# A vision-transformer tower on one Trainium2 core: VectorE normalises directly behind the first two row maxima of a step, and GpSimd splits two patch tiles at the end of step 5

## The chip, the cores and the metric

The kernel is one program on one core of a Trainium2 chip. The metric is device time in microseconds (us). PE is TensorE, DVE is VectorE, ACT is ScalarE, POOL is GpSimd and SP is SyncE, which here only issues DMAs. Each engine works through its own instructions in order; semaphores tie the engines together.

## What is computed

```python
patches = _patchify(x)                                   # 64 images, 196 patches of 768
h = einsum('bnf,ef->bne', patches, W_tok) + b            # to 192 features
xn = layernorm(layernorm(h)) * ln_g + ln_b
q, k, v = split(xn @ qkv_w.T + qkv_b)                    # 12 heads of 16
attn = einsum('bhnd,bhmd->bhnm', q, k) * 16 ** -0.5
attn = attn - 0.2 * (sum of the 8 neighbours in the 196 x 196 plane)
h = h + einsum('bhnm,bhmd->bhnd', softmax(attn), v)
...
h = h + experts(layernorm(h))                            # 8 experts, the best 2 per row, 768 hidden
```

## The kernel before, in words

There are two phases. The attention phase takes the images in 32 pairs. The expert phase behind it routes the rows and multiplies them by the experts' weights; the change does not touch it.

**Steps.** A pair has 6 steps, k = 0 to 5: two images times three groups of four heads. Two pairs are one body, whose steps are kk = 0 to 11; bodies 2 to 13 are a hardware loop, the others are written out. "Even pair" below is the one of kk 0 to 5, "odd pair" that of kk 6 to 11. In kk 8, 9 and 11 a body also splits a part of the experts' weights (`stage` to `pack`): ScalarE the high part, VectorE (L838, L840) and GpSimd (L1266) the low parts. Several steps are in flight. In step kk the engines do, in this order:

- TensorE: the scores of heads 0 and 1 of step kk+2 (L635, into `s_bank`); `mix`, probabilities times v of step kk-1 (L664); `transpose_back` of step kk-2 (L617, into `m_bank`); the scores less their maximum of step kk, heads 0 and 1 (L651, `t_bank`); the scores of heads 2 and 3 (L635); a piece of another pair's projections; L651 for heads 2 and 3; `transpose_max` (L675), which turns the maxima of step kk+1 into rows; and once more a piece of projections. In k = 5 that last piece is `project_qk` of the pair after next (L580 to L584): 15 matmuls of 392 columns in three blocks, with nothing between them and the scores of the next step.
- VectorE: `row_maxima` of heads 0 and 1 of step kk+2 (two L859); a piece that depends on k; `normalise` of step kk-2 (L882 the reciprocal of the sums, L886 the product into `att`); `row_maxima` of heads 2 and 3; `split_maxima` (L867 and L870); another piece that depends on k.
- ScalarE: exponentials (L1060), copies out of PSUM and the high parts of splits (`x_hi` L1038, `x_ah` L1090, `x_b` L1092, `padded` L1104, `qk_hi` L1113).
- GpSimd: k = 0 `beside` (L1236) and patch tile 3; k = 1 `sum_rows`; k = 3 patch tile 0, `inverse_deviation` (L1201 to L1207) and `layernorm` (L1212, L1218); k = 4 patch tile 1, `inverse_deviation_n` (L1248 to L1255) and `low_rows` (L1261); k = 5 patch tile 2; kk = 11 also L1266. A patch tile is one `split_patches` (L1228, `x_lo` from `x_buf` and `x_hi`).

**Three ties matter.** `transpose_max` writes the bank that `normalise` reads, so it waits in each step for that step's L886 (`att_ready`). `project_qk` waits for `split_low` (`x_split`): VectorE's L927 and L928 of step 5. `split_low` waits for `x_high`, ScalarE's L1090 and L1092 of the end of step 4:

```python
pe.wait_ge(max_parts_ready, st.s + 1)      # transpose_max
wait(pe, att_ready, st.s - 2)
...
pe.wait_ge(x_split, 4 * (pr.u + 1))        # project_qk, block 0
...
dve.wait_ge(x_high, 2 * (pr.u + 1))        # split_low
```

SP stores and stacks q and k between k = 1 and k = 3 of a pair; the change moves no DMA in SP's queue, and GpSimd issues none in this phase.

Of the kernel before, what the change touches and what calls it, by code (L numbers as in the profile page):

```python
# [84 lines left out]
def wait(eng, sem, value):  # L85

    if not isinstance(value, int) or value > 0:
        eng.wait_ge(sem, value)
# [66 lines left out]
def attention_phase(nc, x_t, w_tok, w_qk_a, w_qk_b, w_v_a, w_v_b, b_tok, b_qk, b_v, ln_cols, row_consts, ident_in,  # L155
# [4 lines left out]
    with ctx:  # L160
# [6 lines left out]
        def sem(name):  # L167
            return ctx.enter_context(nc.semaphore(name))
# [113 lines left out]
        x_split = sem("x_split")  # L282
# [465 lines left out]
        def _(dve):  # L748
# [106 lines left out]
            def row_maxima(st, heads):  # L855
                if st.there:
                    for hh in heads:
                        dve.wait_ge(s_ready, HG * st.s + hh + 1)
                        nc.vector.reduce_max(row_max[st.odd][:, :, hh:hh + 1], s_bank[hh % 2][0:HALF, :, 0:TOKENS],  # L859
                                             AX.X).then_inc(max_ready, 1)  # L860
# [13 lines left out]
            def normalise(st):  # L874

                if st.there:
                    dve.wait_ge(back_ready, st.s + 1)
                    wait(dve, att_ready, st.s)
                    if st.first:
                        wait(dve, y_stored[st.q], 16 * st.before)  # L880
                        wait(dve, xn_n_ready, TILES * (st.pair - 1))
                    nc.vector.reciprocal(recip[:], back_tr[:, :, :, HEAD_DIM:HEAD_DIM + 1]).then_inc(recip_ready, 1)  # L882
                    dve.wait_ge(recip_ready, st.s + 1)
                    width = HG * HEAD_DIM
                    out = att[st.q][:, 2 * st.image:2 * st.image + 2, st.group * width:(st.group + 1) * width]
                    nc.vector.tensor_tensor(out.rearrange("p u (h d) -> p u h d", h=HG),  # L886
                                            back_tr[:, :, :, 0:HEAD_DIM],
                                            recip[:].to_broadcast([HALF, 2, HG, HEAD_DIM]), ALU.mult
                                            ).then_inc(att_ready, 1)
# [33 lines left out]
            def split_low(pr):  # L923

                if pr.there:
                    dve.wait_ge(x_high, 2 * (pr.u + 1))
                    nc.vector.tensor_tensor(x_al[:], xt_a[:], x_ah[:], ALU.subtract).then_inc(x_split, 2)  # L927
                    nc.vector.tensor_tensor(x_b[HI:P, :], xt_b[HI:P, :], x_b[HI:P, :], ALU.subtract  # L928
                                            ).then_inc(x_split, 2)
# [39 lines left out]
            def fill_pipeline():  # L969

                first, second = Pair(0, 0, 0), Pair(0, 0, 1)
                for half in range(2):
                    take_h(first, half)
                    statistics(first, half)
                take_xt_a(first)
                split_low(first)
                for half in range(2):
                    take_h(second, half)
                    statistics(second, half)
                add_tilde(first)  # L980
                take_v(first, 0)
                take_v(first, 1)
                take_low_plain(first)
                take_low_tilde(first)
                take_xt_a(second)
                split_low(second)
                set_up_rows()

            def step(body, kk):
                k = kk % STEPS  # L990
                if kk == -FILL:
                    fill_pipeline()
                row_maxima(Step(body, kk, LOOK), (0, 1))
                if kk >= 0:
                    if k == 1:
                        take_low_plain(Pair(body, kk, 1))
                    elif k == 2:
                        take_h(Pair(body, kk, 2), 0)
                        statistics(Pair(body, kk, 2), 0)
                    elif k == 4:  # L1000
                        take_v(Pair(body, kk, 1), 0)
                        take_v(Pair(body, kk, 1), 1)
                    elif k == 5:
                        split_low(Pair(body, kk, 2))
                normalise(Step(body, kk, -2))
                row_maxima(Step(body, kk, LOOK), (2, 3))
                split_maxima(Step(body, kk, LOOK))
                if kk >= 0:
                    if k == 0:
                        add_tilde(Pair(body, kk, 1))  # L1010
                    elif k == 1:
                        take_low_tilde(Pair(body, kk, 1))
                    elif k == 2:
                        take_h(Pair(body, kk, 2), 1)
                        statistics(Pair(body, kk, 2), 1)
                    elif k == 3:
                        statistics_n(Pair(body, kk, -1))
                    elif k == 4:
                        take_xt_a(Pair(body, kk, 2))
                    if kk == 11:  # L1020
                        low_part(body)
                    if kk == 4 and isinstance(body, int) and body == 1:
                        split_biases()
                    if kk == 10 and isinstance(body, int) and body == 0:
                        prepare_router()
# [169 lines left out]
        def _(pool):  # L1195
# [26 lines left out]
            def split_patches(pr, tiles):  # L1222

                if pr.there:
                    for tile in tiles:
                        cols = slice(tile * HALF, (tile + 1) * HALF)
                        pool.wait_ge(x_hi_ready, TILES * pr.u + tile + 1)
                        nc.gpsimd.tensor_tensor(x_lo[:, :, cols], x_buf[pr.q][:, :, cols], x_hi[:, :, cols],  # L1228
                                                ALU.subtract).then_inc(x_lo_ready[tile // 2], 1)
# [27 lines left out]
            def low_rows(pr):  # L1257
                if pr.there:
                    pool.wait_ge(row_hi_ready, pr.u + 1)
                    wait(pool, row_stored[pr.q], 16 * pr.before)  # L1260
                    nc.gpsimd.tensor_tensor(row[pr.q][:, :, DIM:XROW], xn_n[:], row[pr.q][:, :, 0:DIM], ALU.subtract  # L1261
                                            ).then_inc(row_lo_ready, 1)
# [6 lines left out]
            def step(body, kk):  # L1269
                k = kk % STEPS  # L1270
                if kk == -FILL:
                    first, second = Pair(0, 0, 0), Pair(0, 0, 1)
                    split_patches(first, (0, 1, 2, 3))
                    split_patches(second, (0, 1))
                    pool.wait_ge(consts_set, CONSTS)
                    inverse_deviation(first)
                    layernorm(first)
                    split_patches(second, (2, 3))
                    add_beside(first)
                    inverse_deviation(second)  # L1280
                    layernorm(second)
                    pool.wait_ge(setup_n, 4)
                    nc.gpsimd.affine_select(router.before[:], router.ones[:], [[1, P]], ALU.is_gt, 0.0, base=0,
                                            channel_multiplier=-1).then_inc(before_set, 1)
                if k == 0:
                    add_beside(Pair(body, kk, 1))
                    if Pair(body, kk, 1).there:
                        pool.wait_ge(tilde_ready, Pair(body, kk, 1).u + 1)
                    split_patches(Pair(body, kk, 2), (3,))
                elif k == 1:  # L1290
                    if Pair(body, kk, 1).there:
                        pool.wait_ge(plain_lo_ready, Pair(body, kk, 1).u + 1)
                    sum_rows(Pair(body, kk, -1))
                elif k == 3:
                    split_patches(Pair(body, kk, 3), (0,))
                    if kk >= 0:
                        inverse_deviation(Pair(body, kk, 2))
                        layernorm(Pair(body, kk, 2))
                elif k > 3:
                    split_patches(Pair(body, kk, 3), (k - 3,))  # L1300
                    if kk >= 0 and k == 4:
                        inverse_deviation_n(Pair(body, kk, -1))
                        low_rows(Pair(body, kk, -2))
                if kk == 11:
                    low_part(body)
            run_bodies(pool, step)


# [727 lines left out]
```

## Time and profile before

| | us |
|---|---|
| median of three runs (lowest, highest) | 2218.97 (2218.96, 2224.03) |
| the profiled execution | 2227.03 |
| its span | 2225.0 |
| PE, DVE busy | 1889.0 (85%), 1496.4 (67%) |
| ACT, POOL busy | 1274.4 (57%), 1136.7 (51%) |
| granted TensorE clock, mean | 0.922 |

The shares are means over two unlike phases. The attention phase ends near 1250 us of the span and the expert phase takes up its speed near 1400 us. A granted clock of 1.00 is 2.4 GHz, 0.50 is 1.2 GHz.

### The profile page before, as it was taken

To read this page: it belongs to the slowest core of one execution; us is meant where nothing else is said; L and a number is where in the kernel's file an instruction comes from. 1 tells how busy PE (TensorE), PEld (TensorE's weight loads), DVE (VectorE), ACT (ScalarE), POOL (GpSimd) and SP (SyncE) were. 2 spreads that over 40 slices of the span, in tenths; PEclk is the share of its full clock that TensorE was granted. 3 is DMA by queue.
4 is the path that set the end of the run, shared out by engine and by line. 5 is a ranking of instruction groups with operands and counts; after the bars stand their busy time and mean duration, and the time that the engine had idled before them with its cause. 6 is when DMAs were issued, how large, how long until landed. Compare 5 with 4: busy or idle time off the path is not lost. (4 is left out here: it accounts for less than half of the span.)

```text
span 2225.0 us, 54385 instructions
## 1 busy us (share of the span) xinstructions
PE 1889.0 (85%) x17949; PEld 1396.1 (63%) x17949; DVE 1496.4 (67%) x4652; ACT 1274.4 (57%) x2469; POOL 1136.7 (51%) x1069
## 2 busy tenths in 40 slices
PE   4878888888888878788888657999999999999991
PEld 4655565656565656565655445777777777777761
DVE  4768787888788888888888534655655655654430
ACT  4657777777777777777777623444444444433330
POOL 4335454444545454545453234666676676664442
PEclk8889999999999999999998756999999999999996
DMA  4565555555556454645463326887888888789886
GB/s 151 159 192 160 161 178 157 176 162 165 170 155 183 143 176 157 185 143 169 160 184 114 112 85 163 200 190 201 214 189 208 209 188 207 197 198 176 187 165 191
DMA packets 362727, 382.72 MB, mean 172 GB/s; under 512 B 144532, under 2 KB 326096, under 8 KB 358288
## 3 DMA queue, kind: packets, MB, share of 16 engines
q1 hardware_dynamic: 320912, 338.66, 52.1%
q0 software_dynamic: 41664, 42.12, 11.2%
q8 instruction: 86, 1.41, 0.3%
q14 instruction: 65, 0.53, 0.1%
HBM read 232.83 MB, written 135.46 MB: 166 GB/s over the span
## 5 line engine op out<-in xcount | busy, mean ns | idle before, releaser
L859 DVE TENSOR_REDUCE row_max<-s_bank 98x2 f32<-98x392 f32 x768 | 395.3, 557 | 110.0 <-PE s_bank L635 109.6
L1790 DVE SCALAR_TENSOR_TENSOR ml<-mid_bank,mh 128x512 bf16<-128x512 f32 x336 | 232.1, 691 | 329.3 <-ACT mh L1878 328.2
L1878 ACT ACTIVATE mh<-mid_bank 128x512 bf16<-128x512 f32 x336 | 200.7, 597 | 409.4 <-PE mid_bank L1569 409.4
L1060 ACT ACTIVATE probs<-t_bank 98x392 f32<-98x392 f32 x768 | 342.5, 503 | 121.2 <-PE t_bank L651 119.6
L1944 POOL DMA_INDIRECT sums<-y_out,tail x168 | 265.2, 1578 | 158.0 <-DVE y_out L1820 110.9
L1586 PE MATMUL y_bank<-wst,ml 128*128 128x192 bf16 x1344 | 330.1, 246 | 0.0
L1583 PE MATMUL y_bank<-wst,mh 128*128 128x192 bf16 x1344 | 330.1, 246 | 0.0
L1585 PE MATMUL y_bank<-wst,mh 128*128 128x192 bf16 x1344 | 329.9, 245 | 0.0
L1228 POOL TENSOR_TENSOR x_lo<-x_buf,x_hi 128x588 f16<-128x588 f32 x128 | 172.0, 1346 | 298.2 <-ACT x_hi L1038 234.0
L635 PE MATMUL s_bank<-k_stack,q_stack 96*98 96x196 f16 x1536 | 224.4, 257 | 48.7 <-DVE row_max L859 38.0
L651 PE MATMUL t_bank<-q_stack,k_stack 104*98 104x196 f16 x1536 | 224.2, 258 | 40.2 <-ACT probs L1060 36.5
L1929 POOL DMA_INDIRECT slots<-row_r,spot x196 | 191.2, 975 | 98.8 <-issue 56.4
L635 PEld LDWEIGHTS s_bank<-k_stack,q_stack 96*98 96x98 f16 x1536 | 145.2, 126 | 92.9 <-DVE row_max L859 84.5
L543 PE MATMUL p_bank<-wtok_h,x_hi 128*98 128x192 f16 x768 | 192.8, 251 | 10.6 <-POOL x_lo L1228 10.3
L651 PEld LDWEIGHTS t_bank<-q_stack,k_stack 104*98 104x98 f16 x1536 | 149.3, 126 | 79.7 <-ACT probs L1060 77.4
L1077 ACT COPY q_stack<-m_bank 8x784 f16<-8x784 f16 x192 | 154.6, 805 | 74.7 <-PE m_bank L675 70.7
L544 PE MATMUL p_bank<-wtok_l,x_hi 128*98 128x192 f16 x768 | 191.9, 250 | 0.0
L545 PE MATMUL p_bank<-wtok_h,x_lo 128*98 128x192 f16 x768 | 191.9, 250 | 0.0
L664 PE MATMUL o_bank<-probs,v_buf 98*32 98x196 f32 x3072 | 172.0, 342 | 7.3 <-ACT probs L1060 3.2
L1236 POOL TENSOR_TENSOR beside<-padded 128x1176 f32<-128x1176 f32 x32 | 68.7, 2147 | 214.0 <-ACT padded L1104 214.0
L1583 PEld LDWEIGHTS y_bank<-wst,mh 128*128 128x128 bf16 x1344 | 134.4, 100 | 24.9 <-issue 5.3
L675 PE MATMUL m_bank<-ident,max_parts 98*128 98x98 f16 x384 | 50.1, 213 | 111.2 <-DVE att L886 109.5
(236 smaller groups left out, 4682.7 us busy)
## 6 DMA issues: line engine op xcount, KB each, us to landing
wst<-packed SPq DMA_DIRECT2D x56, 1584.0 KB
x_buf<-in_x_t SPq DMA_DIRECT2D x32, 1176.0 KB, 7.6
q_stack<-stack_parts SPq DMA_DIRECT2D x288, 98.0 KB, 2.5
k_stack<-stack_parts SPq DMA_DIRECT2D x288, 98.0 KB, 2.6
stack_parts<-qk_hi SPq DMA_DIRECT2D x32, 588.0 KB, 2.9
stack_parts<-qk_lo SPq DMA_DIRECT2D x32, 588.0 KB, 3.1
sums<-h_buf SPq DMA_DIRECT2D x32, 294.0 KB
h_in<-sums SPq DMA_DIRECT2D x32, 294.0 KB
```

What stands on the lines that cost most here:

```text
L543: nc.tensor.matmul(out, x_hi[:, f, tokens], wtok_h[:, f, :], start=(f == 0), stop=False)
L544: nc.tensor.matmul(out, x_hi[:, f, tokens], wtok_l[:, f, :], start=False, stop=False)
L635: last = nc.tensor.matmul(s_bank[hh % 2][0:HALF, u, 0:TOKENS], q_stack[st.q][0:PARTS, head, head_cols(st, u)], k_stack[st.q][0:PARTS, head ...
L651: last = nc.tensor.matmul(out, k_stack[st.q][:, head, head_cols(st, v)], q_stack[st.q][:, head, head_cols(st)], start=True, stop=True)
L859: nc.vector.reduce_max(row_max[st.odd][:, :, hh:hh + 1], s_bank[hh % 2][0:HALF, :, 0:TOKENS], AX.X).then_inc(max_ready, 1)
L1060: nc.scalar.activation(probs[st.odd][:, hh], t_bank[hh % 2][0:HALF, :, 0:TOKENS], ACT.Exp).then_inc(probs_ready, 1)
L1583: nc.tensor.matmul(o, mh[n % MID][:, cols], high, start=(c == 0 and j % 2 == 0), stop=False, skip_group_check=True)
L1585: nc.tensor.matmul(o, mh[n % MID][:, cols], low, start=False, stop=False, skip_group_check=True)
L1586: last = nc.tensor.matmul(o, ml[n % MID][:, cols], high, start=False, stop=False, skip_group_check=True)
L1790: nc.vector.scalar_tensor_tensor(ml[n % MID][:], mid_bank[n % MID_PS][:], 0.0, mh[n % MID][:], ALU.max, ALU.subtract).then_inc(ml_ready, 1)
L1878: nc.scalar.activation(mh[n % MID][:], mid_bank[n % MID_PS][:], ACT.Relu).then_inc(mh_ready, 1)
L1944: nc.gpsimd.indirect_dma_start(out=total_rows, out_offset=bass.IndirectOffsetOnAxis(ap=to, axis=0), in_=y_out[q][:, j, :], in_offset=None, ...
```

## The change

VectorE's `normalise` moves ahead of the piece that depends on k (k = 1, 2, 4 and 5 have one there). GpSimd's tile 0 moves from k = 3 to k = 4, and tiles 1 and 2 both stand in k = 5 behind a new wait for `x_split`.

```diff
                 row_maxima(Step(body, kk, LOOK), (0, 1))
+                normalise(Step(body, kk, -2))
                 if kk >= 0:
                     if k == 1:
                         take_low_plain(Pair(body, kk, 1))
...
                     elif k == 5:
                         split_low(Pair(body, kk, 2))
-                normalise(Step(body, kk, -2))
                 row_maxima(Step(body, kk, LOOK), (2, 3))
...
                 elif k == 3:
-                    split_patches(Pair(body, kk, 3), (0,))
                     if kk >= 0:
                         inverse_deviation(Pair(body, kk, 2))
                         layernorm(Pair(body, kk, 2))
-                elif k > 3:
-                    split_patches(Pair(body, kk, 3), (k - 3,))
-                    if kk >= 0 and k == 4:
+                elif k == 4:
+                    split_patches(Pair(body, kk, 3), (0,))
+                    if kk >= 0:
                         inverse_deviation_n(Pair(body, kk, -1))
                         low_rows(Pair(body, kk, -2))
+                elif k == 5:
+                    if kk >= 0 and Pair(body, kk, 2).there:
+                        pool.wait_ge(x_split, 4 * (Pair(body, kk, 2).u + 1))
+                    split_patches(Pair(body, kk, 3), (1, 2))
```

VectorE, step 5 of a pair (`recip` and `att` are normalise, `x_al` and `x_b` split_low):

```order
 L859 TENSOR_REDUCE row_max<-s_bank 98x2 x2
+L882 RECIPROCAL recip<-m_bank 98x8
+L886 TENSOR_TENSOR att<-m_bank,recip 98x2x64
 L927 TENSOR_TENSOR x_al<-xt_a,x_ah 128x392
 L928 TENSOR_TENSOR x_b<-xt_b,x_b 64x392
-L882 RECIPROCAL recip<-m_bank 98x8
-L886 TENSOR_TENSOR att<-m_bank,recip 98x2x64
 L859 TENSOR_REDUCE row_max<-s_bank 98x2 x2
 L867 TENSOR_SCALAR max_parts<-row_max 98x2x4
```

Both instructions of normalise now stand ahead of both of split_low; nothing else changes place.

VectorE, step 1 (L956 is the low part of q and k):

```order
 L859 TENSOR_REDUCE row_max<-s_bank 98x2 x2
+L882 RECIPROCAL recip<-m_bank 98x8
+L886 TENSOR_TENSOR att<-m_bank,recip 98x2x64
 L956 TENSOR_TENSOR qk_lo<-padded,qk_hi 128x1176
-L882 RECIPROCAL recip<-m_bank 98x8
-L886 TENSOR_TENSOR att<-m_bank,recip 98x2x64
 L859 TENSOR_REDUCE row_max<-s_bank 98x2 x2
 L867 TENSOR_SCALAR max_parts<-row_max 98x2x4
```

There normalise moves ahead of L956, which waits for ScalarE's L1113.

GpSimd in the loop, the start of step 3 and the end of step 5 of the even pair (`x_lo` is a patch tile; the register and ISA rows belong to the waits):

```order
 L1243 TENSOR_TENSOR att<-att,h_in 98x768
-L1227 ISA
-L1228 TENSOR_TENSOR x_lo<-x_buf,x_hi 128x6x98
+L1199 ISA
 L1201 TENSOR_TENSOR var_eps<-meanvar,one_eps 98x4
 L1203 ISA
...
 L88 ISA
 L1261 TENSOR_TENSOR row<-xn_n,row 98x4x192
+L1227 REGISTER_ALU
+L1228 TENSOR_TENSOR x_lo<-x_buf,x_hi 128x6x98
 L1227 REGISTER_ALU
 L1228 TENSOR_TENSOR x_lo<-x_buf,x_hi 128x6x98
```

One patch tile has left step 3, and two stand behind L1261 where one stood; the tile between L1218 and L1248 in step 4 is now tile 0.

## Rows read from the trace of the kernel before

**Rows 1.** Windows: length, busy PE, PEld, DVE, ACT, POOL, clock, DMA share, GB/s.

```profile
200.00:1250.00 1050.00, 874.16 (x9185) 636.77 (x9182) 872.19 (x2153) 793.16 (x1536) 494.76 (x503) 0.94 0.53 163
865.30:868.70 3.40, 0.51 (x4) 0.26 (x4) 3.30 (x5) 1.28 (x3) 2.10 (x2) 1.00 0.69 207
868.70:872.20 3.50, 3.50 (x13) 1.66 (x12) 0.98 (x4) 1.48 (x2) 0.00 (x0) 0.51 0.91 335
1199.90:1203.30 3.40, 1.85 (x22) 0.92 (x14) 3.27 (x5) 1.80 (x6) 1.15 (x1) 1.00 0.62 174
1203.30:1206.70 3.40, 3.03 (x12) 1.49 (x13) 3.23 (x10) 2.04 (x4) 0.00 (x0) 0.50 0.01 3
```

**Rows 2.** Waits of 200 to 1250 us (total, times, longest), and line L928 there.

```profile
PE m_bank L675 <- DVE att L886: 100.4, 55, 3.1
...
L928 DVE TENSOR_TENSOR x_b<-xt_b,x_b x27: 565/1526/1557, 224.2 to 1203.3; 64x392 bf16<-64x392 f32 x27
```

**Rows 3.** Timeline of PE, even pair: start, length, what, and idle before.

```profile
864.88 0.76 PE L651 MATMUL t_bank<-q_stack,k_stack 104*98 104x196 f16 x4 [0.27 <-ACT probs L1060]
868.53 0.25 PE L675 MATMUL m_bank<-ident,max_parts 98*128 98x98 f16 x2 [2.89 <-DVE att L886]
...
872.91 0.50 PE L635 MATMUL s_bank<-k_stack,q_stack 96*98 96x196 f16 x4
```

**Rows 4.** Timeline of PE, odd pair of the same body.

```profile
903.13 0.76 PE L651 MATMUL t_bank<-q_stack,k_stack 104*98 104x196 f16 x4 [0.97 <-ACT probs L1060]
906.95 0.32 PE L675 MATMUL m_bank<-ident,max_parts 98*128 98x98 f16 x2 [3.06 <-DVE att L886]
...
910.90 0.50 PE L635 MATMUL s_bank<-k_stack,q_stack 96*98 96x196 f16 x4
```

**Rows 5.** Timeline of DVE, steps 4 and 5 of the even pair.

```profile
861.72 0.63 DVE L867 TENSOR_SCALAR max_parts<-row_max 98x8 f16<-98x8 f32 x1
...
863.16 1.03 DVE L859 TENSOR_REDUCE row_max<-s_bank 98x2 f32<-98x392 f32 x2
864.32 1.92 DVE L927 TENSOR_TENSOR x_al<-xt_a,x_ah 128x392 bf16<-128x392 f32 x1
866.26 1.56 DVE L928 TENSOR_TENSOR x_b<-xt_b,x_b 64x392 bf16<-64x392 f32 x1
...
868.10 0.29 DVE L886 TENSOR_TENSOR att<-m_bank,recip 98x128 f32<-98x128 f32 x1
```

**Rows 6.** Timeline of DVE, steps 1, 3 and 5 of the odd pair.

```profile
880.31 1.39 DVE L956 TENSOR_TENSOR qk_lo<-padded,qk_hi 128x1176 f16<-128x1176 f32 x1 [1.15 <-ACT qk_hi L1113]
...
893.86 0.17 DVE L867 TENSOR_SCALAR max_parts<-row_max 98x8 f16<-98x8 f32 x1
...
902.56 2.12 DVE L927 TENSOR_TENSOR x_al<-xt_a,x_ah 128x392 bf16<-128x392 f32 x1 [1.09 <-ACT x_b L1092]
```

**Rows 7.** Timeline of POOL, steps 3 to 5, even pair; the last row odd pair.

```profile
854.41 1.31 POOL L1228 TENSOR_TENSOR x_lo<-x_buf,x_hi 128x588 f16<-128x588 f32 x1 [7.46 <-ACT x_hi L1038]
...
864.17 1.65 POOL L1261 TENSOR_TENSOR row<-xn_n,row 98x768 f16<-98x768 f32 x1
865.77 1.63 POOL L1228 TENSOR_TENSOR x_lo<-x_buf,x_hi 128x588 f16<-128x588 f32 x1
...
904.22 1.59 POOL L1266 TENSOR_TENSOR pack<-stage,pack 128x576 bf16<-128x576 f32 x1
```

**Rows 8.** Timeline of DVE and POOL in the last pair with a `split_low`.

```profile
1193.29 0.79 DVE L867 TENSOR_SCALAR max_parts<-row_max 98x8 f16<-98x8 f32 x1
...
1199.88 1.20 DVE L870 SCALAR_TENSOR_TENSOR max_parts<-row_max,max_parts 98x8 f16<-98x8 f32 x1
...
1202.74 0.57 DVE L927 TENSOR_TENSOR x_al<-xt_a,x_ah 128x392 bf16<-128x392 f32 x1
...
1192.58 1.47 POOL L1212 TENSOR_TENSOR centred<-h_buf,meanvar 98x768 f32<-98x768 f32 x1
...
1199.78 1.28 POOL L1266 TENSOR_TENSOR pack<-stage,pack 128x576 bf16<-128x576 f32 x1
```

## The prediction, made before the changed kernel ran

> **What bounds the kernel now.** I read four views, in this order. The windows say where to look: in the 1050 us from 200 to 1250 no engine is full (PE 874, DVE 872, ACT 793 us busy), and the DMA engines are busy for 0.53 of it [rows 1]. So no engine's throughput sets the pace there, a chain across engines does. The waits name its most visible link: PE waits 55 times and 100.4 us in total for VectorE's L886, at most 3.1 us at a time [rows 2]. L928 gives the number of pairs: 27 in that stretch, all at about 1.5 us except one of 0.57 us, so 26 pairs run in the pattern that follows [rows 2].
>
> The timeline of PE shows the link in time. In step 5 of the even pair PE ends L651 at 864.88 + 0.76 = 865.64, waits 2.89 us, does L675 at 868.53, and then `project_qk` until the next scores at 872.91 [rows 3]. In the odd pair the same places are 903.89, 3.06, 906.95 and 910.90 [rows 4]. Scores to scores is 910.90 - 872.91 = 37.99 us. Behind this wait everything stands in line: the row maxima of the next step need those scores, and the next step's work hangs on them. A microsecond taken out of this wait is therefore a microsecond of the pair, as long as nothing else ends last in it.
>
> The timeline of VectorE says what fills the wait. L927 takes 1.92 us and L928 1.56 us [rows 5]. In the last pair L927 takes 0.57 us with GpSimd silent [rows 8], and the one short L928 is 0.565 us [rows 2]. The ends tell why: GpSimd's L1261 runs to 864.17 + 1.65 = 865.82 and its patch tile to 867.40 [rows 7], and VectorE's two end at 866.24 and 867.82 [rows 5], each 0.42 us after one of these. VectorE stands still while GpSimd's instruction runs. In the odd pair L927 takes 2.12 us [rows 6].
>
> **The change part by part.** I cost it in place, pair by pair.
>
> *Normalise ahead of split_low.* In step 5 both are needed before `project_qk` can start, so the order alone gives little: L675 is free 3 us sooner, but the first block of `project_qk` then waits for L928. The normalise costs 867.82 to 868.39, so 0.57 us, and it is now ahead of L927.
>
> *Patch tiles behind x_split.* The tile leaves step 3, so GpSimd's whole row from there comes 1.31 us sooner [rows 7]; tile 0 takes the place of tile 1 in step 4. L1261 thus ends at 865.82 - 1.3 = 864.5 instead of 865.82, and the tile that held L928 can't start before L928 has ended. So L927 and L928 cost 0.57 + 0.03 + 0.57 = 1.17 us.
>
> *Step 1.* Normalise goes into a wait of 1.15 us ahead of L956 [rows 6]. It takes 0.5 us out of VectorE's row behind L956. The instructions of L956's many waits may then run a little later, so I take 0.34 us of gain, with bounds 0 and 0.57. Cover: the wait for ScalarE's L1113; if it were gone the gain would be nothing.
>
> *Steps 2 and 4.* The same work in another order on an engine that has no wait there: nothing, as long as `transpose_back` is done by then. It stands straight behind `mix` on PE, and in neither step does a row of waits show VectorE waiting at L882.
>
> *Step 3, a new collision.* GpSimd's L1212 now comes 1.31 us sooner against VectorE, which puts it on L867. The last pair, which has no tile in step 3, shows exactly this: L1212 runs 1192.58 to 1194.05, and L867 takes 0.79 instead of 0.17 us [rows 6, 8]. Price: 0.62 us.
>
> *Step 4, a collision that goes.* L867 takes 0.63 us beside the tile of step 4 [rows 5]; that tile is gone by then, and 0.46 us come back.
>
> The sum for VectorE up to step 5: -0.34 + 0.62 - 0.46 = -0.18 us.
>
> *Even pair.* Row maxima end at 864.19 [rows 5], less 0.18, plus 0.57 for normalise, plus 1.17: 865.75. PE is there at 865.64 - 0.34 = 865.3, does L675 in 0.25, and begins `project_qk` near 865.8. Before it began at 868.53 + 0.25 = 868.78. Gain: 2.97 us. L1261 must be done when L927 starts at 864.6: its end at 864.5 less 0.34 leaves 0.4 us.
>
> *Odd pair.* L927 waited 1.09 us for ScalarE [rows 6], and normalise hides in that. L928 ends at 902.56 - 0.34 + 1.17 = 903.4, and PE ends L651 at 903.89 - 0.34 = 903.55, then L675. PE is now last: `project_qk` begins at 903.9, before at 907.27. Gain: 3.35 us.
>
> *What comes late next.* Two tiles and in the odd pair L1266 stand behind `x_split`: 903.5 + 1.3 + 1.3 + 1.59 = 907.7 us. VectorE's L867 and L870, and in kk 11 L838 and L840, fall into them. L870 took 1.20 us beside L1266 [rows 8], so they are caught. In the even pair this ends at 868.5, well before the next row maxima. In the odd pair VectorE is free only near 908.8, while `project_qk` would end near 907.5. PE has `mix`, `transpose_back` and the first L651 to do before it needs the result, so I charge 0.4 us per odd pair, nearer to the lower of the bounds 0 and 1.3 (908.8 less 907.5).
>
> The Trainium skill says in "SBUF — State Buffer", section "Who interferes with whom", that of a two-input VectorE instruction and a GpSimd one the second to issue blocks until the first has ended. By that the change moves collisions as well as removing them, and this speaks for the 0.62 and the 0.4 us. The trace agrees with the blocking but not with its length: in the odd pair L927 asked at 902.56 and ended 2.12 us later.
>
> *TensorE's clock.* After the idle stretch in step 5 (0.51 of 3.40 us busy) the granted clock is 0.51 for the next 3.50 us, so 1.2 GHz, and `project_qk` falls into it [rows 1]. Fully at 2.4 GHz its 4.13 us (868.78 to 872.91) would be about 3.0; in the even pair 1.15 us are to be had, in the odd pair about 0.3, since VectorE's tail is the last there. Against it stands the last pair: PE was busy for 1.85 of 3.40 us, and still the clock fell to 0.50 [rows 1]. In the changed step 5 PE would still be idle for 0.97 us ahead of L651 in the odd pair [rows 4], which lies between the two cases and full work. The bounds are 0 and 13 x 1.45 = 19 us; I take 11.
>
> The Trainium skill, "TensorE: Matmul & The Clock Gate", section "HAM oscillation — how this bites in real kernels", tells that a wait once a tile makes the clock fall again in each tile. By it all 19 us would come back with the wait, and the total would be 8 us better than mine.
>
> **Sum.** 13 x 2.97 + 13 x 3.35 = 82.2; less 13 x 0.4 = 5.2; plus 11: 88 us. The six other pairs have no such overlap or a different pattern, and I give them nothing. Against the profiled execution: 2227.0 - 88 = 2139 us. The median of before lies 8.1 us below that execution, so 2219 - 88 = 2131 us.
>
> **The rivals.** *L1261 still meets L927* (0.10). The margin is 0.4 us, and if VectorE gets ahead by more, L927 waits for L1261 to end and takes up to 1.9 us. For: the margin is small. Against: the two come out of the same chain, and ScalarE's L1092 holds L927 in the odd pair. The gain would then be about 1.6 us an even pair and 2.5 an odd one: 13 x 4.1 = 53, so 2166 us.
>
> *The clock comes back in full and stays* (0.25). The gain is 82 + 19 - 5 = 96 us, 2123 us; with early pairs joining in at 3 us each it reaches 108, so 2111 us.
>
> *The chain is not the bound* (0.04): a DMA ends last when the pair is shorter, and the time stays within 0.3% of 2219. For: their share is 0.91 in a stretch of 3.50 us [rows 1]. Against: a mean share of 0.53 leaves room [rows 1], and the waits name no DMA.
>
> *Slower* (0.03): VectorE's tail behind the two tiles and L1266. It decides if VectorE is still blocked when the next scores are done and the whole saved time and more is spent there: L867 would have to come free 3.4 us later than 908.8, in each odd pair, and in the even pair 4 us later than 868.5. By rows it would need GpSimd's instructions to keep VectorE out for twice their length. At 1 us beyond that point a pair the time would be 2219 + 26 = 2245 us.
>
> **How the numbers follow.** The forecast as such has 0.58: its range is 2120 to 2148, from the bounds of step 1, tail and clock. The full clock adds 0.25, the L1261 rival 0.10, no change 0.04, slower 0.03. To hold 8 in 10 with some room for a term that I mis-sized the range is 2108 to 2166 us. This kernel can tell about 0.3% (7 us) from no change. Faster 0.93, same 0.04, slower 0.03.
>
> **What would show it.** L927 and L928 near 0.57 us in both pairs; L867 of step 3 at 0.8 us; PE waiting in step 5 for L928 in the even pair for about 0.2 us and hardly in the odd; L867 or L870 of step 5 at over 1 us; scores to scores near 34.5 us; the stretch at 1.2 GHz gone in about half of the pairs. Wrong would be a PE wait of over 1 us in step 5, a new wait of PE for `x_lo`, or a longer row of VectorE in steps 1 to 4.

## The result, and the profile after

| | before | after |
|---|---|---|
| median (lowest, highest), four runs each | 2218.97 (2216.52, 2224.03) us | 2121.22 (2119.23, 2124.20) us |
| ratio, 95% interval | | 0.9558 [0.9536, 0.9580] |
| profiled execution, its span | 2227.03, 2225.0 us | 2124.2, 2122.0 us |
| granted TensorE clock, mean | 0.922 | 0.941 |

The kernel is faster by 97.8 us. The forecast was 2131 us with a range of 2108 to 2166 us.

First the windows of the changed kernel (length, busy time of PE, PEld, DVE, ACT and POOL, clock, DMA share, GB/s). The first answers to the first of [rows 1]; the others are the ends of step 5 and the starts of `project_qk`, in an odd and an even pair:

```profile
200.00:1150.00 950.00, 834.63 (x9162) 625.15 (x9160) 867.88 (x2154) 785.99 (x1536) 493.20 (x502) 0.99 0.59 180
764.00:765.40 1.40, 0.74 (x7) 0.52 (x8) 1.27 (x3) 1.40 (x4) 0.01 (x1) 1.00 0.81 215
765.40:768.80 3.40, 2.69 (x18) 1.44 (x17) 3.33 (x6) 2.98 (x6) 3.40 (x3) 1.00 0.88 313
797.10:798.90 1.80, 1.50 (x12) 0.74 (x10) 1.70 (x6) 1.80 (x6) 0.39 (x1) 1.00 0.80 241
798.90:802.30 3.40, 2.81 (x17) 1.56 (x18) 2.65 (x4) 2.88 (x6) 2.57 (x2) 1.00 0.94 289
```

The last row stands against the third of [rows 1]: the same matmuls, now at 2.4 GHz, where the granted clock was 0.51. DVE is busy for 0.91 of the long stretch (867.88 of 950), before for 0.83; this counts the time in which it stands still beside GpSimd.

The waits of the same stretch (total, times, longest). The wait of L675 for L886 [rows 2], 100.4 us, has no row any more:

```profile
POOL var_eps L1201 <- DVE meanvar L914: 205.3, 27, 8.3
ACT probs L1060 <- PE t_bank L651: 117.7, 87, 4.8
PEld s_bank L635 <- DVE row_max L859: 103.5, 215, 1.9
...
PE s_bank L635 <- DVE row_max L859: 47.9, 58, 1.7
```

The last row is PE's largest wait now. Before it was half of that (200 to 1250 us):

```profile
PE s_bank L635 <- DVE row_max L859: 25.3, 56, 1.2
```

So a part of the time taken out of step 5 has come back as a wait of PE for VectorE's row maxima. Its long ones are one in nearly every pair, of 1.3 to 1.4 us, in step 2.

PE's timeline, first the odd pair and then the even one, which answer to [rows 4] and [rows 3]:

```profile
734.80 0.50 PE L635 MATMUL s_bank<-k_stack,q_stack 96*98 96x196 f16 x4
...
764.64 0.76 PE L651 MATMUL t_bank<-q_stack,k_stack 104*98 104x196 f16 x4 [0.97 <-ACT probs L1060]
765.24 0.25 PE L675 MATMUL m_bank<-ident,max_parts 98*128 98x98 f16 x2
765.39 0.33 PE L580 MATMUL p_bank<-x_ah,wqk_ah 128*128 128x392 bf16 x1
...
767.92 0.34 PE L580 MATMUL p_bank<-x_ah,wqk_ah 128*128 128x392 bf16 x1 [0.71 <-ACT padded L1104]
...
768.76 0.50 PE L635 MATMUL s_bank<-k_stack,q_stack 96*98 96x196 f16 x4
...
798.05 0.76 PE L651 MATMUL t_bank<-q_stack,k_stack 104*98 104x196 f16 x4 [0.27 <-ACT probs L1060]
798.64 0.25 PE L675 MATMUL m_bank<-ident,max_parts 98*128 98x98 f16 x2
798.92 0.34 PE L580 MATMUL p_bank<-x_ah,wqk_ah 128*128 128x392 bf16 x1
...
801.33 0.34 PE L580 MATMUL p_bank<-x_ah,wqk_ah 128*128 128x392 bf16 x1 [0.58 <-ACT padded L1104]
...
802.16 0.50 PE L635 MATMUL s_bank<-k_stack,q_stack 96*98 96x196 f16 x4
```

Scores to scores is 33.96 us in the odd pair and 33.40 us in the even one; the odd pair had 37.99. L675 follows L651 without a wait, and `project_qk` follows L675. Inside `project_qk` a wait is new: ahead of its third block PE stands for 0.71 and 0.58 us until ScalarE's L1104 has copied a block out of PSUM.

VectorE's timeline of the odd pair, steps 1 to 5 and the start of the next pair (answers to [rows 5, 6]):

```profile
742.20 1.38 DVE L956 TENSOR_TENSOR qk_lo<-padded,qk_hi 128x1176 f16<-128x1176 f32 x1 [0.33 <-issue]
...
744.56 1.10 DVE L867 TENSOR_SCALAR max_parts<-row_max 98x8 f16<-98x8 f32 x1
...
755.44 0.78 DVE L867 TENSOR_SCALAR max_parts<-row_max 98x8 f16<-98x8 f32 x1
...
761.17 0.20 DVE L867 TENSOR_SCALAR max_parts<-row_max 98x8 f16<-98x8 f32 x1
...
764.07 0.57 DVE L927 TENSOR_TENSOR x_al<-xt_a,x_ah 128x392 bf16<-128x392 f32 x1 [0.42 <-ACT x_b L1092]
764.67 0.56 DVE L928 TENSOR_TENSOR x_b<-xt_b,x_b 64x392 bf16<-64x392 f32 x1
...
766.34 0.40 DVE L867 TENSOR_SCALAR max_parts<-row_max 98x8 f16<-98x8 f32 x1
766.77 1.22 DVE L870 SCALAR_TENSOR_TENSOR max_parts<-row_max,max_parts 98x8 f16<-98x8 f32 x1
767.91 0.55 DVE L838 SCALAR_TENSOR_TENSOR pack<-stage,pack 128x384 f16<-128x384 f32 x1
768.38 1.63 DVE L840 SCALAR_TENSOR_TENSOR pack<-stage,pack 64x384 f16<-64x384 f32 x1
769.94 1.02 DVE L859 TENSOR_REDUCE row_max<-s_bank 98x2 f32<-98x392 f32 x2
```

and GpSimd beside it (answers to [rows 7]):

```profile
754.73 1.47 POOL L1212 TENSOR_TENSOR centred<-h_buf,meanvar 98x768 f32<-98x768 f32 x1
...
761.60 1.65 POOL L1261 TENSOR_TENSOR row<-xn_n,row 98x768 f16<-98x768 f32 x1
765.39 2.57 POOL L1228 TENSOR_TENSOR x_lo<-x_buf,x_hi 128x588 f16<-128x588 f32 x2 [2.15 <-DVE x_b L928]
767.92 1.68 POOL L1266 TENSOR_TENSOR pack<-stage,pack 128x576 bf16<-128x576 f32 x1
```

Read the two together. GpSimd is silent from 763.25 to 765.39, and L927 and L928 fall into that silence. Several of VectorE's instructions that start while GpSimd's large ones run are stretched: L867 of step 3 beside L1212, L867 and L870 behind `split_low` beside the tiles, and L840 beside L1266. Not all are: L859 and L838, which fall beside such instructions too, keep their 1.02 and 0.55 us.

### The profile page after: what moved, and what is told of

Read it like the earlier page. It is cut to its first block and busy times, and to the rows that moved or that the text cites. A ratio compares the mean times of both kernels' runs of the same rounds, so it can differ in the third digit from the quotient of the medians.

```text
span 2122.0 us, 54414 instructions
## 1 busy us (share of the span) xinstructions
PE 1845.8 (87%) x17949; PEld 1383.3 (65%) x17949; DVE 1494.5 (70%) x4652; ACT 1267.0 (60%) x2469; POOL 1136.7 (54%) x1069
## 5 line engine op out<-in xcount | busy, mean ns | idle before, releaser
L859 DVE TENSOR_REDUCE row_max<-s_bank 98x2 f32<-98x392 f32 x768 | 395.2, 557 | 34.3 <-PE s_bank L635 32.7
L635 PE MATMUL s_bank<-k_stack,q_stack 96*98 96x196 f16 x1536 | 232.9, 258 | 82.8 <-DVE row_max L859 68.0
L651 PE MATMUL t_bank<-q_stack,k_stack 104*98 104x196 f16 x1536 | 220.1, 256 | 37.3 <-ACT probs L1060 34.9
L1228 POOL TENSOR_TENSOR x_lo<-x_buf,x_hi 128x588 f16<-128x588 f32 x128 | 166.4, 1312 | 157.8 <-DVE tilde L947 66.9
L651 PEld LDWEIGHTS t_bank<-q_stack,k_stack 104*98 104x98 f16 x1536 | 149.4, 126 | 71.7 <-ACT probs L1060 69.2
L1586 PEld LDWEIGHTS y_bank<-wst,mh 128*128 128x128 bf16 x1344 | 134.3, 100 | 24.9 <-issue 5.3
L1588 PEld LDWEIGHTS y_bank<-wst,mh 128*128 128x128 bf16 x1344 | 131.1, 98 | 20.0
L1947 POOL DMA_INDIRECT sums<-y_out,dest x56 | 86.9, 1552 | 97.1 <-DMA sums<-y_out,dest 46.7
```

What stands on the lines that cost most here:

```text
L635: last = nc.tensor.matmul(s_bank[hh % 2][0:HALF, u, 0:TOKENS], q_stack[st.q][0:PARTS, head, head_cols(st, u)], k_stack[st.q][0:PARTS, head ...
L651: last = nc.tensor.matmul(out, k_stack[st.q][:, head, head_cols(st, v)], q_stack[st.q][:, head, head_cols(st)], start=True, stop=True)
L1586: nc.tensor.matmul(o, mh[n % MID][:, cols], high, start=(c == 0 and j % 2 == 0), stop=False, skip_group_check=True)
L1588: nc.tensor.matmul(o, mh[n % MID][:, cols], low, start=False, stop=False, skip_group_check=True)
L1947: nc.gpsimd.indirect_dma_start(out=total_rows, out_offset=bass.IndirectOffsetOnAxis(ap=to, axis=0), in_=y_out[q][:, j, :], in_offset=None, ...
```

## The experiments

The first four ran together on one chip, the next four together on one chip. On both the kernel before is slower than above (2236.11 and 2233.69 us), so ratios are compared, not times. The traces show where the chips differ. The attention phase can be measured by L1236, which runs once a pair; the table has one traced execution of each kernel, in us. From the start of the last L1236 to the end it takes 1013 to 1014 us in the first two rows and 1023 to 1030 in the others, whatever the kernel. So the attention phase can be compared across chips (e5 and the changed kernel, which are the same, differ by 2.4 us there), to a few us.

| kernel | last L1236 starts | 26 pairs, sixth L1236 to last | of this at the low clock | from the last L1236 to the end |
|---|---|---|---|---|
| before | 1210.6 | 978.6 | 99.0 | 1014.4 |
| changed | 1108.8 | 886.0 | 20.5 | 1013.2 |
| e1 | 1170.3 | 939.9 | 75.1 | 1028.0 |
| e2 | 1109.8 | 887.2 | 3.4 | 1026.2 |
| e3 | 1171.6 | 939.8 | 71.7 | 1025.1 |
| e4 | 1101.2 | 878.5 | 23.9 | 1022.8 |
| e5 | 1106.4 | 884.2 | 17.1 | 1028.9 |
| e6 | 1072.5 | 850.8 | 0 | 1026.9 |
| e7 | 1105.9 | 885.4 | 30.7 | 1024.3 |
| e8 | 1069.6 | 850.0 | 0 | 1029.9 |

**e1_normalise_alone.** VectorE's half of the change.

```diff
                 row_maxima(Step(body, kk, LOOK), (0, 1))
+                normalise(Step(body, kk, -2))
...
-                normalise(Step(body, kk, -2))
                 row_maxima(Step(body, kk, LOOK), (2, 3))
```

> Only VectorE's normalise moves; GpSimd stays as before. Theory (the gain is VectorE no longer standing still beside GpSimd in L927 and L928): these two still take about 1.9 and 1.5 us, only L675 leaves the path, some 1.2 us a pair and 26 pairs: about 2187 us. Rival (the order of normalise is the gain, since PE's wait was named after L886): about 2121 us, as the full change.

Measured: 2202.01 us, ratio 0.9869 [0.9839, 0.9898], 29 us at the scale of 2219 where 32 were expected. VectorE in the odd and the even pair:

```profile
802.30 2.13 DVE L927 TENSOR_TENSOR x_al<-xt_a,x_ah 128x392 bf16<-128x392 f32 x1 [0.50 <-ACT x_b L1092]
804.46 1.52 DVE L928 TENSOR_TENSOR x_b<-xt_b,x_b 64x392 bf16<-64x392 f32 x1
...
838.66 1.68 DVE L927 TENSOR_TENSOR x_al<-xt_a,x_ah 128x392 bf16<-128x392 f32 x1
840.37 1.55 DVE L928 TENSOR_TENSOR x_b<-xt_b,x_b 64x392 bf16<-64x392 f32 x1
```

In the odd pair the two are as long as before; in the even one L927 takes 1.68 instead of 1.92 us, since it is asked for nearer to the end of L1261. The 26 pairs are 38.7 us shorter than before, and a part of that is the clock: at the start of `project_qk` it is low in about one pair of two, where before it was in each. The rival falls: PE's wait was named after L886, but L886 was only the last of what stood in VectorE's queue.

**e2_tiles_alone.** GpSimd's half, with normalise behind `split_low` as before.

```diff
                 elif k == 3:
-                    split_patches(Pair(body, kk, 3), (0,))
...
-                elif k > 3:
-                    split_patches(Pair(body, kk, 3), (k - 3,))
+                elif k == 4:
+                    split_patches(Pair(body, kk, 3), (0,))
...
+                elif k == 5:
+                    if kk >= 0 and Pair(body, kk, 2).there:
+                        pool.wait_ge(x_split, 4 * (Pair(body, kk, 2).u + 1))
+                    split_patches(Pair(body, kk, 3), (1, 2))
```

> Only GpSimd's patch tiles move, with the wait for x_split; normalise stays behind split_low. Theory: L927 and L928 take 0.57 us each, but normalise and L675 stay on the path: 2.3 to 2.55 us a pair, with some of the clock 80 to 90 us in all: about 2135 us. Rival (order of normalise is the gain): near 2200 us.

Measured: 2140.62 us, ratio 0.9585 [0.9567, 0.9602], 92 us at the scale of 2219, just above the expected 80 to 90. L927 and L928 take 0.57 and 0.56 us, and L675 still waits 0.55 us for L886 in the even pair:

```profile
798.57 0.25 PE L675 MATMUL m_bank<-ident,max_parts 98*128 98x98 f16 x2 [0.55 <-DVE att L886]
```

GpSimd's half makes nearly all of the gain. The full change had 0.9558 and, beside the second four, 0.9597, so what normalise adds on top isn't resolved by these intervals. The traces tell why it is so little. Between two L1236, most pairs of e2 take 33.8 and 34.4 us and those of the full change 33.3 and 34.05, so normalise in front does shorten a pair by some 0.4 us. `project_qk` starts 1.1 us earlier in the even pair (30.16 against 31.27 us after the pair's first scores), but 0.6 us of that goes into its wait for L1104, which e2 all but lacks: there it takes 2.60 us in place of 3.24.

```profile
798.79 0.33 PE L580 MATMUL p_bank<-x_ah,wqk_ah 128*128 128x392 bf16 x1
...
801.39 0.50 PE L635 MATMUL s_bank<-k_stack,q_stack 96*98 96x196 f16 x4
```

And e2 has no wait of PE over 1.2 us in these pairs and almost no low clock (3.4 us), where the changed kernel has 20.5 us. The two effects cancel: the 26 pairs take 887.2 us in e2 and 886.0 and 884.2 with the full change.

**e3_no_wait_for_x_split.** The full change without the wait.

```diff
                 elif k == 5:
-                    if kk >= 0 and Pair(body, kk, 2).there:
-                        pool.wait_ge(x_split, 4 * (Pair(body, kk, 2).u + 1))
                     split_patches(Pair(body, kk, 3), (1, 2))
```

> The full change without GpSimd's wait for x_split, so that tiles 1 and 2 follow L1261 at once. Theory: in the trace of the changed kernel L1261 ends 0.2 us (even pair) and 0.8 us (odd) before L927 starts, so a tile would be running then and L927 and L928 take 3 us together again: 1.2 to 2.5 us a pair lost, about 2170 us. Rival (enough that the row of GpSimd comes 1.3 us sooner; the wait is not needed): 2121 us.

Measured: 2200.51 us, ratio 0.9860 [0.9836, 0.9884]. That is e1 again. VectorE, GpSimd and PE in an odd pair:

```profile
796.54 2.13 DVE L927 TENSOR_TENSOR x_al<-xt_a,x_ah 128x392 bf16<-128x392 f32 x1 [0.42 <-ACT x_b L1092]
798.70 1.52 DVE L928 TENSOR_TENSOR x_b<-xt_b,x_b 64x392 bf16<-64x392 f32 x1
```

```profile
794.06 1.65 POOL L1261 TENSOR_TENSOR row<-xn_n,row 98x768 f16<-98x768 f32 x1
795.67 2.57 POOL L1228 TENSOR_TENSOR x_lo<-x_buf,x_hi 128x588 f16<-128x588 f32 x2
798.20 1.59 POOL L1266 TENSOR_TENSOR pack<-stage,pack 128x576 bf16<-128x576 f32 x1
```

```profile
800.27 0.34 PE L580 MATMUL p_bank<-x_ah,wqk_ah 128*128 128x392 bf16 x1 [2.32 <-DVE x_b L928]
801.45 0.53 PE L580 MATMUL p_bank<-x_ah,wqk_ah 128*128 128x392 bf16 x1
```

GpSimd's earlier row alone brings nothing beyond e1 (26 pairs in 939.8 and 939.9 us); the wait does. It isn't needed for any data: it only keeps GpSimd silent for the 1.2 us in which VectorE is on the path. And with PE's wait of 2.32 us the low clock is back in the odd pairs: the L580 of the second block takes 0.53 us, as before the change, where it takes 0.33 us in the changed kernel. In the even pair behind it PE waits 1.93 us and the clock stays full.

**e4_tile_0_in_step_3.** The full change with the tile of step 4 back in step 3.

```diff
                 elif k == 3:
+                    split_patches(Pair(body, kk, 3), (0,))
                     if kk >= 0:
                         inverse_deviation(Pair(body, kk, 2))
                         layernorm(Pair(body, kk, 2))
                 elif k == 4:
-                    split_patches(Pair(body, kk, 3), (0,))
```

> The full change, but patch tile 0 back at the head of step 3, which takes L1212 off VectorE's L867. Theory: L867 of step 3 falls from 0.78 to 0.17 us, but L927 then has to wait for L1261 in the even pair and for ScalarE in the odd one, so at most 0.2 us a pair comes through: 2116 to 2121 us. Rival (VectorE's row in steps 1 to 4 is the bound throughout): 0.6 us a pair, 2105 us.

Measured: 2134.37 us, ratio 0.9564 [0.9538, 0.9590], the full change's. VectorE in steps 3, 4 and 5 of an even pair, and GpSimd:

```profile
853.48 0.17 DVE L867 TENSOR_SCALAR max_parts<-row_max 98x8 f16<-98x8 f32 x1
...
861.04 0.74 DVE L927 TENSOR_TENSOR x_al<-xt_a,x_ah 128x392 bf16<-128x392 f32 x1
```

```profile
859.71 1.65 POOL L1261 TENSOR_TENSOR row<-xn_n,row 98x768 f16<-98x768 f32 x1
```

The 0.6 us of step 3 are saved, and in the even pair L927 then meets the end of L1261 (861.36) and waits. Pairs without a low clock take 33.04 and 34.05 us from L1236 to L1236, with the full change 33.34 and 34.05: so 0.3 us comes through in one pair of two, nothing in the other. The attention phase is 5 to 8 us shorter than in e5 and the changed kernel, which the ratio doesn't resolve. The theory holds.

**e5_full_change_again.** No edit.

> The full change once more, as the yardstick for the three beside it on the same chip: the ratio measured at first, 0.956 of before, within its interval.

Measured: 2141.06 us, ratio 0.9597 [0.9575, 0.9619]. It overlaps the first interval only at its edge (0.9575 to 0.9580), so the same kernel differs by 0.004 between two chips. By the table the difference lies behind the attention phase. The three below are compared with this one.

**e6_sum_rows_after_L966.**

```diff
                 elif k == 1:
                     if Pair(body, kk, 1).there:
-                        pool.wait_ge(plain_lo_ready, Pair(body, kk, 1).u + 1)
+                        pool.wait_ge(tilde_lo_ready, Pair(body, kk, 1).u + 1)
                     sum_rows(Pair(body, kk, -1))
```

> The full change, and GpSimd's sum_rows (L1243) waits in step 1 for the low part of tilde (L966) in place of that of plain (L956). In the changed kernel L867 of step 1 takes 1.10 us beside L1243. Theory (a stop of VectorE beside GpSimd costs its full length wherever VectorE's row is on the path): L867 at 0.17 us, 0.9 us a pair, 24 us: ratio to before 0.945. Rival (step 1 is paced by ScalarE and TensorE): 0.956.

Measured: 2099.91 us, ratio 0.9406 [0.9385, 0.9427], 41 us below e5 where 24 were expected. VectorE in step 1 of an odd pair, and GpSimd:

```profile
721.71 0.18 DVE L867 TENSOR_SCALAR max_parts<-row_max 98x8 f16<-98x8 f32 x1
```

```profile
724.11 1.81 POOL L1243 TENSOR_TENSOR att<-att,h_in 98x768 f32<-98x768 f32 x1 [5.71 <-DVE qk_lo L966]
```

L867 takes 0.18 instead of 1.10 us. The mechanism holds and the size was too small. By the traces the 26 pairs fell by 33.4 us. Of that, 26 times 0.92 us are 24. The rest is the clock: e5 has five pairs with a stretch at the low clock, each 1.5 to 1.8 us longer than the others of its kind, and e6 has none. With it goes the long wait of PE in step 2, which is 1.3 or 1.4 us in nearly each pair of e5 and at most 0.7 us in e6, since L867 stands ahead of the row maxima that PE waits for. That the shorter wait keeps the clock up is argued from this and from e2, not tried apart. The 41 us of the medians are more than the 36 us between the two traced spans, and a part of them isn't placed.

**e7_tile_2_in_step_0.**

```diff
                 if k == 0:
...
-                    split_patches(Pair(body, kk, 2), (3,))
+                    split_patches(Pair(body, kk, 2), (2, 3))
...
-                    split_patches(Pair(body, kk, 3), (1, 2))
+                    split_patches(Pair(body, kk, 3), (1,))
```

> The full change, and patch tile 2 moves on from step 5 to step 0, beside tile 3. It is the price of VectorE's tail (L867, L870, L838, L840 behind two tiles and L1266, ending at 770.0 us where the scores of the next step start at 768.8). Theory: the tail ends 1.2 us sooner in the odd pair and 0.4 us or so of that comes through, 5 us in all; the second tile in step 0 takes 0.2 to 0.4 us of it back at L956: ratio 0.954 to 0.957. Rival (the tail is a full loss of 1.2 us in the odd pairs): 16 us, ratio 0.949.

Measured: 2132.16 us, ratio 0.9547 [0.9527, 0.9566], 0.005 below e5, intervals not overlapping by a little. Inconclusive for its question: the attention phase is as long in both traces (the last L1236 starts at 1105.9 against 1106.4 us), so nearly all of the 5.1 us between their spans lies in the expert phase, which differs by as much between kernels that are alike there. The rival's 16 us are not there.

**e8_e4_e6_e7_together.**

> The three variants together: tile 0 in step 3, sum_rows behind L966, tile 2 in step 0. Theory: the sum of their effects, ratio 0.942 to 0.945, since they touch three different places of the pair. Rival: one chain of ScalarE and TensorE ends last once VectorE is free, and it stops at 0.950.

Measured: 2099.82 us, ratio 0.9399 [0.9380, 0.9418]: e6, and nothing more. It lies just below the expected 0.942 to 0.945, since e6 alone had given more than expected; e4 and e7 add nothing to it that shows (26 pairs in 850.0 and 850.8 us). The rival's 0.950 is not there either. e6 and e8 are the fastest kernels here.

## Why the prediction was right

**The bound.** The wait of PE in step 5 was VectorE standing still beside GpSimd. Right: where L927 and L928 are short it is gone (0.55 us are left in the row of e2), and where they are long PE waits for them, by 1.9 to 2.4 us (e1, e3).

**L927 and L928 at 1.17 us together.** 0.57 and 0.56 us in the pairs shown, and L927 at 0.55 to 0.57 us in all. Right.

**The lead of L1261 over L927.** Taken as 0.4 us; in the even pair L1261 ends at 797.49 and L927 starts at 797.71, so 0.2 us. That rival came close, and e4 shows what it costs when it begins to happen, 0.17 us at L927.

**Step 1, gain 0.34 us.** L956 starts 7.40 us after the scores (742.20 less 734.80) as before (880.31 less 872.91), its wait filled, and normalise's time is gone behind it: the gain is 0.44 us at the next row maxima and 0.38 us at L927 of step 5. Right in size. I left out L867 of this step, which takes 1.02 us before the change (883.12 us) and 1.10 after, beside L1243; of the things tried here, e6 shows, this was the largest left.

**Step 3, price 0.62 us; step 4, 0.46 us back.** L867 takes 0.78 us in step 3 and 0.20 us in step 4. Right. But the sentence on two-input instructions that I put behind the 0.62 us doesn't reach L867, which has one tensor as input (`max_parts<-row_max`); what carried this price was the row of the last pair.

**The tail, 0.4 us in odd pairs.** VectorE is busy until 770.01 us, 1.25 us after the scores; I had 1.3. What comes through is the difference in the first step: L956 starts 7.71 us after the scores behind the odd pair (776.47 less 768.76) and 7.40 behind the even one, so 0.31 us.

**The clock, 11 us.** Two parts, and the sum is smaller than I took. `project_qk` to scores went from 4.13 to 3.24 us in the even pair and from 3.63 to 3.37 in the odd one, so 13 x 1.15 = 15 us came back, of at most 19. All its matmuls now run at full clock, one every 0.166 us, 2.5 us for the 15; what keeps it above the 3.0 us that I gave the even pair is the wait for L1104, which I had not seen. Against this, six pairs have a low stretch somewhere else, and are about 1.7 us longer than their neighbours, 10 us in all:

```profile
678.91 1.03 PE L635 MATMUL s_bank<-k_stack,q_stack 96*98 96x196 f16 x4 [1.43 <-DVE row_max L859]
```

```profile
675.60:679.00 3.40, 1.97 (x28) 1.25 (x27) 3.04 (x5) 2.86 (x6) 0.77 (x1) 1.00 0.45 177
679.50:682.50 3.00, 3.00 (x20) 3.00 (x21) 2.69 (x8) 0.00 (x0) 0.00 (x0) 0.51 0.90 282
```

Each of the six begins within 0.8 us behind the end of PE's wait for the row maxima in step 2, as here (windows, columns as above). That wait is in nearly every pair, so why only six fall isn't settled. So the clock gave some 5 us net in place of 11, although its low stretches went from one in each pair to six in the 26, where I had expected half of them to stay. The rule that I cited from the Trainium skill, "TensorE: Matmul & The Clock Gate", section "HAM oscillation — how this bites in real kernels", would have given all 19 us, which this trace does not bear out.

**What was mis-sized upward.** The 26 pairs gave 92.6 us (978.6 before, 886.0 after) where I had 88. The odd pair's part ahead of `project_qk` fell by 3.77 us (from 34.36 to 30.59) and not by 3.35. I had let L675 wait for the whole 0.76 us of L651 and `project_qk` start 0.35 us later; in the trace they start 0.60 and 0.15 us behind one another. The even pair's part fell by 2.86 us with the tail in it (from 33.02 to 30.16). Together this is 13 x (3.77 + 2.86) = 86 us where I had 77; with 5 us of the clock it makes 91. The first pairs, priced at nothing, gave 9.2 us by the sixth L1236. With 1.2 us at the end this is the 103 us between the spans.

**What was luck.** The mechanism of step 5 was right, but the total is nearer than its terms: the row was 9 us too small, the clock 6 us too large, and the first pairs 9 us that I had at nothing. And the number alone would not have told my forecast from the rival with the full clock: 2121 us lies 1 us inside my 2120 to 2148, and within the 2111 to 2123 of that rival. The traces decide it: the clock did not stay full.

## What to carry to other kernels

When one of VectorE's instructions has one length in most pairs and a third of it in a few, compare its ends with GpSimd's: an end that is always the same 0.4 us behind a GpSimd instruction was a stop here, not work. The remedy can be a wait that no data needs: GpSimd kept silent for the microsecond in which VectorE is on the path, with its work moved to where VectorE waits anyway. And a wait named after the last instruction of a queue says where to look, not what to move: moving that one (e1) gave 0.013, where the full change gave 0.040 and 0.044. Then look for the next wait: here a part of the gain went into PE's wait in step 2 and into ScalarE's L1104, and shortening the first of these was worth another 0.019 (e6).

## What the runs showed of the hardware beyond that

VectorE doesn't always get in when GpSimd's instruction ends. L927, asked for 0.39 to 0.47 us ahead of such an end with another GpSimd instruction right behind, was passed over and waited for the second one too (the odd pairs of before and e1 and nearly all of e3, 2.08 to 2.16 us); asked for 1.05 us or more ahead (their even pairs) it got in, and GpSimd's next one was late (1.62 to 1.64 instead of 1.31 us [rows 7]). With nothing of GpSimd right behind, 0.31 us ahead was enough (e4, 0.74 us). L867, asked for 0.36 us ahead, did get in (0.40 us at 766.34) and L870 behind it did not (1.22 us). What decides this wasn't tried. And a GpSimd instruction that is long by the trace need not stop VectorE: before the change L867 and L870 of step 3 take 0.17 us each (893.86 and 894.06 us) inside GpSimd's L1207, 98x4 in 1.02 us (893.51 us).
